# Slot weights in two halves: one batch of 8 matmuls ahead of a projection, the other behind it

## The reference

```python
xn = _layernorm(x, axis=-1)
q, k = _rope(hs @ Wq.T), _rope(hs @ Wk.T)       # per head, T = 256, DK = 128
A  = where(mask, einsum('bhtd,bhjd->bhtj', q, k) * scale, 0)
ok = enz * einsum('bhtj,bhjm->bhtm', A, es)     # es = exp(s), enz = exp(-cumlogsumexp(s)), m = 64 slots
qv = softmax(ok, axis=-1)
W2 = where(mask, einsum('bhtm,bhjm->bhtj', qv * enz, es), 0)
o  = einsum('bhtj,bhjd->bhtd', W2, v)
o_n = o * rsqrt(mean(o * o) + EPS) * g_norm_weight
out = (o_n * silu(hs @ Wg.T)) @ Wo.T
# ffn: gate, up and down projections with 4-bit weights and a tanh GELU
```

## Time and profile before

| | us |
|---|---|
| median of 3 runs | 1122.98 |
| lowest and highest | 1122.49, 1124.65 |
| the profiled execution's own time | 1122.49 |
| its span, first to last instruction | 1120.0 |
| mean granted TensorE clock, as a share of full speed | 0.985 |
| PE busy | 1084.0 (97%) |
| DVE busy | 928.1 (83%) |
| ACT busy | 650.6 (58%) |
| POOL busy | 425.5 (38%) |

### The profile page before, as it was taken

The page is one execution under the profiler, slowest core; times in us unless marked ns, Lnnn a source line. Parts: engine busy times, 40 slices in busy tenths (PEclk is TensorE's granted clock), DMA queues, the critical chain, the costliest instruction groups (busy, mean ns, idle before and its releaser), DMA issues.

```text
span 1120.0 us, 20624 instructions
## 1 busy us (share of the span) xinstructions
PE 1084.0 (97%) x7176; PEld 927.7 (83%) x7176; DVE 928.1 (83%) x1687; ACT 650.6 (58%) x2103; POOL 425.5 (38%) x308
## 2 busy tenths in 40 slices
PE   6888999999999999999999999999999999999996
PEld 5677888888888888888888888888888888888875
DVE  6788889888888889888888888888888898888863
ACT  4465566655655657555666656565665556655542
POOL 7142245432524345232453324443252334523231
PEclk9899999999999999999999999999999999999996
DMA  4002000020002000020000200011000200000001
GB/s 166 1 1 78 1 2 1 2 77 1 1 1 78 1 2 1 1 78 1 1 1 1 78 1 2 1 38 41 1 1 1 78 1 1 1 1 20 1 20 38
DMA packets 9526, 23.06 MB, mean 21 GB/s; under 512 B 848, under 2 KB 5840, under 8 KB 8528
## 3 DMA queue, kind: packets, MB, share of 16 engines
q1 hardware_dynamic: 9424, 21.76, 5.4%
HBM read 19.66 MB, written 2.10 MB: 19 GB/s over the span
## 4 chain that ended last, share of the span: by engine, by line
PE 84%; DVE 7%; issue 4%; POOL 2%; ACT 2%; DMA 0%; POOLq 0%; DVEq 0%; ACTq 0%
PE bank L205 20%; PE bank L207 19%; PE bank L206 19%; PE bank L303 4%; PE bank L366 4%; PE bank L316 3%; PE bank L337 3%; DVE xs L930 2%; PE bank L375 2%; PE bank L305 2%; PE bank L328 1%; PE bank L529 1%; PE bank L346 1%; PE bank L319 1%; PE bank L359 1%
## 5 line engine op out<-in xcount | busy, mean ns | idle before, releaser
L1200 POOL TENSOR_TENSOR inter_lo<-ffb,inter_hi 128x512 fp32r<-128x512 f32 x64 | 83.3, 1325 | 440.5 <-ACT inter_hi L678 440.5
L1191 POOL TENSOR_TENSOR qkT<-ra,xs 128x512 f32<-128x512 f32 x128 | 170.2, 1329 | 109.6 <-DVE xs L930 80.8
L640 ACT ACTIVATE sm<-bank,mx 128x64 f32<-128x64 f32 x256 | 76.5, 326 | 120.6 <-DVE mx L886 120.6
L930 DVE TENSOR_TENSOR xs<-xs,rope 128x512 f32<-128x512 f32 x128 | 129.5, 1012 | 0.0
L927 DVE TENSOR_TENSOR ra<-bank,rope 128x512 f32<-128x512 f32 x128 | 87.7, 685 | 46.9 <-ACT xs L622 44.7
L621 ACT ACTIVATE xs<-bank 64x512 f32<-64x512 f32 x128 | 76.2, 595 | 66.8 <-PE bank L207 43.8
L205 PE MATMUL bank<-xh,wqk_hi 128*128 128x512 f32 x256 | 109.9, 429 | 3.1 <-DVE h L990 2.6
L875 DVE RECIPROCAL enzT<-enzT 128x256 f32<-128x256 f32 x64 | 111.4, 1742 | 0.0
L205 PE MATMUL bank<-xh,wgu_hi 128*128 128x512 f32 x256 | 105.6, 412 | 0.0
L645 ACT ACTIVATE At<-bank 128x128 f32<-128x128 f32 x128 | 35.8, 281 | 114.1 <-DVE At L809 112.9
L205 PE MATMUL bank<-wvg_hi,xh 128*128 128x512 f32 x256 | 101.1, 395 | 1.0 <-DVE xl L978 1.0
(11 more groups left out here) (149 smaller groups left out, 3075.5 us busy)
## 6 DMA issues: line engine op xcount, KB each, us to landing
raw<-in_w_qkvg SPq DMA_DIRECT2D x7, 1024.0 KB, 5.0
scaled<-in_w_scaled SPq DMA_DIRECT2D x8, 640.0 KB, 7.1
packed<-in_w_packed SPq DMA_DIRECT2D x8, 384.0 KB, 5.7
acc<-in_x SPq DMA_DIRECT2D x4, 512.0 KB, 8.1
out<-acc SPq DMA_DIRECT2D x3, 512.0 KB, 2.9
raw<-in_w_qkvg SPq DMA_DIRECT2D x2, 512.0 KB, 7.1
out<-acc SPq DMA_DIRECT2D x2, 256.0 KB, 2.1
ws_raw<-in_w_slot SPq DMA_DIRECT2D x8, 48.0 KB, 1.8
```

What stands on the lines that cost most here:

```text
L640: ins = act.activation(sm[:, c], src[:, c], ACT.Exp, bias=mx[:, g:g + 1], accum_out=ssum[:, g:g + 1])
L930: dve.tensor_tensor(two(xs[i % 2][:, :]), two(xs[i % 2][:, :]), sin, ALU.mult).then_inc(sin_done, 1)
L1191: pool.tensor_tensor(qkT[:, i, :], ra[i % 2][:, :], xs[i % 2][:, :], ALU.add).then_inc(roped, 1)
L1200: pool.tensor_tensor(inter[1][e][:, :], ffb[e][:, :], inter[0][e][:, :].bitcast(F32), ALU.subtract).then_inc(inter_lo, 1)
```

## The change

`slot_weights` is called twice in a stage. Each call makes the weights of one batch entry, two token tiles for each of the two heads, and so half of the matmuls. The first call stands between the transposes of `esT` and `project_qk` 2, the second where the whole was, ahead of `carried`. `Wt` is four tiles of 128x256 in place of two of 128x512. Both halves use the first 256 columns of `sc[0]` and `sc[1]`, so PE's second half waits until DVE has read the first; in the last stage alone the second half goes to the banks `pj[2]` and `pj[3]`. DVE masks a half as soon as its place in the order comes: `weight_diagonal` 0 and 1 stand between `rope_sin` 0 and `rope_cos` 1, and 2 and 3 between `rope_sin` 1 and `rope_cos` 2. `W_full` and `W_diag` count in steps of four per stage.

```diff
-        Wt = [sb(f"Wt{h}", [P, NT, P]) for h in range(2)]
+        Wt = [sb(f"Wt{i}", [P, 2, P]) for i in range(4)]
...
+        def weight_bank(st, i):
+            return pj[i] if st == STEPS - 1 and i > 1 else sc[i % 2]
...
-            def slot_weights(st, bp):
-
-                for i in range(NT):
-                    t = slice(i * P, (i + 1) * P)
-                    for h in range(2):
-                        g = slice(h * M, (h + 1) * M)
-                        mm = pe.matmul(sc[h][:, t], esT[bp % 2][g, t], qe[g, t], start=True, stop=True)
-                mm.then_inc(W_full, 1)
+            def slot_weights(st, bp, b):
+
+                t0 = b * T
+                pair = [(weight_bank(st, 2 * b + h), slice(h * M, (h + 1) * M)) for h in range(2)]
+                for tt in range(2):
+                    t = slice(t0 + tt * P, t0 + (tt + 1) * P)
+                    for dst, g in pair:
+                        mm = pe.matmul(dst[:, tt * P:(tt + 1) * P], esT[bp % 2][g, t], qe[g, t], start=True, stop=True)
+                mm.then_inc(W_full, 2)
...
-                pe.wait_ge(W_diag, 2 * st + 1 + h)
+                pe.wait_ge(W_diag, 4 * st + 3 + h)
                 for i in range(NT):
-                    mm = pe.matmul(rg[h][:, i * DV:(i + 1) * DV], Wt[h][:, i, :],
+                    mm = pe.matmul(rg[h][:, i * DV:(i + 1) * DV], Wt[i // 2 * 2 + h][:, i % 2, :],
...
-                        pe.wait_ge(W_diag, 2 * st - 1 + i)
+                        pe.wait_ge(W_diag, 4 * st - 1 + i)
...
+                slot_weights(st, bp, 0)
                 if not last:
                     project_qk(st + 1, nbp, nhp, 2)
-                slot_weights(st, bp)
+                if last:
+                    pe.wait_ge(inter_done, 2 * STEPS)
+                else:
+                    pe.wait_ge(W_diag, 4 * st + 2)
+                slot_weights(st, bp, 1)
                 carried(st, last)
                 if last:
-                    pe.wait_ge(inter_done, 2 * STEPS)
                     pe.wait_ge(inter_lo, 2 * STEPS)
...
-            def weight_diagonal(st, h):
-                dve.wait_ge(W_full, st + 1)
+            def weight_diagonal(st, i):
+                dve.wait_ge(W_full, 4 * st + i + 1)
                 wait(dve, o_full, 2 * st)
-                src = sc[h][:, :].rearrange("p (n t) -> p n t", n=NT)
-                mask = mask_w[:, 0, :].unsqueeze(1).to_broadcast([P, NT, P])
-                dve.tensor_tensor(Wt[h][:, :, :], src, mask, ALU.mult).then_inc(W_diag, 1)
+                src = weight_bank(st, i)[:, 0:2 * P].rearrange("p (n t) -> p n t", n=2)
+                dve.tensor_tensor(Wt[i][:, :, :], src, mask_w[:, :, :], ALU.mult).then_inc(W_diag, 1)
...
-                wait(dve, W_full, n - 1)
+                wait(dve, W_full, 4 * (n - 1))
...
+                weight_diagonal(st, 0)
+                weight_diagonal(st, 1)
                 if not last:
                     rope_cos(st + 1, 1)
                     rope_sin(st + 1, 1)
-                weight_diagonal(st, 0)
-                weight_diagonal(st, 1)
+                weight_diagonal(st, 2)
+                weight_diagonal(st, 3)
```

## The result

| | before | after |
|---|---|---|
| median of 5 runs, us | 1122.98 | 1130.14 |
| lowest and highest, us | 1122.22, 1124.65 | 1129.09, 1133.07 |
| profiled execution, us | 1122.49 | 1129.53 |
| its span, us | 1120.0 | 1127.8 |

The changed kernel is slower, by less than 1%: the ratio is 1.0076, 95% interval 1.0056 to 1.0095, that is +8.5 us (6.3 to 10.7). The medians of the table lie 7.2 us apart. Of 15 executions of the changed kernel seven took 1127.5 to 1130.1 us, eight took 1132.8 to 1134.0 us, and none lies between; the median of the five in the table is one of the lower group, as is the profiled execution. The forecast was +9.2 us on the median, with 1132.2 us and a range of 1127.5 to 1136.5 us.

A forecast was written before the change was run, and what follows sets the result against it. PE's list was taken to bound the kernel; 8.6 us for 22 stages, 0.4 for the seven with bp = 3 and 0.5 for stages 0 and 1 made +9.5 us, median 1132.2 us, range 1127.5 to 1136.5.

The forecast's parts named there:

- What bounds the kernel: Mid-run, a stage lasts as long as PE's list takes to issue: PE busy 32.90 of 32.90 us.
- 0.39 us per visit: PE's added separate visit to the 64-row form between transposes and projection 2 costs 0.39 us beyond its matmuls.
- the step in behind a transpose: On PE, going from transposes into the 64-row form, shown by no row: 0.10 us taken, 0 to 0.20 possible.
- DVE's margin: DVE's first maskings end over 0.4 us before PE reaches its second half of the weights; priced at nothing.
- The stages with the split: Seven bp = 3 stages: PE's later arrival eats 0.33 us of waiting for POOL, leaving 0.06 each, 0.4 us in all.
- The sum inside the run: All terms over the stages together add +9.5 us, all of it inside the span.
- the 22 normal stages: Stages 2 to 30 without the seven of bp = 3: 0.39 us each, 8.6 us in all.
- stages 0 and 1: PE already waits for DVE there, hiding the step in; 0.2 to 0.3 us each remains, 0.5 us in all.
- The last stage: Stage 31: transposes and both halves stand side by side without a projection between, so no second visit; nothing added.
- A: Rival at PE's seams: the visit is cheaper than the rows say, +1 to +2 us, 1124.2 us; chance 0.08.
- B: Rival: PE waits for DVE's maskings, 8.7 us on top, 1140.9 us; chance 0.06.
- C: Rival: DVE's third sine starts before POOL's split, so seven PE waits go, -2.3 us, 1120.7 us; chance 0.04.

The follow-up runs named there:

- e1: Kernel before with PE's order kept and only DVE's two 128x512 maskings cut into four of 128x256 at the old place: 1123.54 us, ratio 1.0007.
- e2: Kernel before with only four of the eight weight matmuls moved ahead of projection 2 on PE, DVE's maskings unchanged: 1132.55 us, ratio 1.0079.
- e3: Kernel before plus one full-height dummy matmul over 128 rows between the transposes and projection 2: 1125.88 us, ratio 1.0030.
- e5: Kernel before with POOL's subtraction for the gate and up weights cut to 128x8 after the first head pair: 1120.30 us, ratio 0.9974.
- e8: Kernel before plus a pair of 64-row dummy matmuls directly behind slot_states, which has the 64-column form: 1136.60 us, ratio 1.0125.
- e7: Kernel before plus a pair of 64-column dummy matmuls over all 128 rows between the transposes and projection 2: 1137.55 us, ratio 1.0128.

## Why the prediction was right

- **What bounds the kernel**: PE's list. e1 and e2 show it: what DVE does in addition costs 0.4 us in the whole run, what PE's order adds is paid in full in every normal stage.
- **0.39 us per visit**: right, 0.39 to 0.40 in every normal stage. The term chosen by the nearest row, 0.10 us for the step in behind a transpose, is some 0.08 us in the profile after. The Trainium skill's rule ("TensorEngine Tiling (Array Packing)", "Tiling Modes", a change of mode drains the engine) agrees with the trace here, with e3 as its control: the price comes with the form and not with the place. A drain as such is not seen in a trace. What the page does not say is the price: 0.39 us there and back for the 64-row form, 0.34 for the 64-column form.
- **DVE's margin**: forecast "over 0.4 us" ahead of PE's second half, measured 0.44. The sine that was held up did swallow the delay.
- **The stages with the split**: this term was mis-sized. Forecast were 0.06 us left of each, +0.4 in all; measured are -0.5. In six of them nothing is left (33.41 us in both kernels in stage 11). The wait was read as 0.33 us; e5 shows that the long period held 0.50 us of cost in all, the part beyond the wait itself lying in slower passes behind it. The seventh, stage 19, was not looked at: it held 0.80 us and lost 0.41 with the change.
- **The sum inside the run**: forecast +9.5 us. The values of stage 30 start at 1070.44 and 1079.45 us, 9.0 apart. This is closer than the terms are: the 22 normal stages give 8.7 (forecast 8.6), the seven others -0.5 (0.4), stages 0 and 1 give 0.3 (0.5), and 0.5 us was there before the first divided group, at the transposes that start at 43.70 and 44.21 us, and has nothing to do with the change; that it fills half of the gap is luck:

```profile
1070.44 0.38 PE L366 MATMUL bank<-vS,Wt 128*128 128x128 f32 x2
```
```profile
1079.45 0.38 PE L370 MATMUL bank<-vS,Wt 128*128 128x128 f32 x2
```

- **The last stage** was forecast at nothing and gave 1.2 us back in this pair of traces (the spans differ by 7.8). This term was mis-sized, and not by the change: PE's clock. Windows over the same work in the last stage, before and after (the column behind POOL's is the granted clock):

```profile
1095.00:1101.00 6.00, 5.22 (x36) 4.59 (x35) 2.35 (x4) 0.00 (x0) 0.00 (x0) 0.51 0.26 87
```
```profile
1104.00:1110.00 6.00, 5.22 (x41) 4.59 (x40) 2.56 (x6) 0.00 (x0) 0.00 (x0) 0.61 0.26 87
```

PE had idled 3.7 us for the softmax just before in both, the clock fell to the lower of its two levels (1.2 GHz), and it came back sooner in the profile after, so that 41 passes in place of 36 start in the window. That is 0.5 us; the other 0.6 come from passes behind two later waits, which run at the lower level in before (from 1109.70 us on, granted clock 0.50 over 3 us) and begin at the upper one in after (from 1118.16 us on). The matmuls and the waits are the same in both, and the five runs of each kernel spread over 2.4 and 4.0 us, so I take this for a matter of the execution. With one trace of each kernel it is not shown. Of the 2.5 us by which the profiled pair (+7.0) stays under the forecast sum, 1.2 lie here, 0.5 in the stages before, and 0.8 outside the span, where the profiled execution of after has 1.7 us and that of before 2.5.
- **The rivals**: A and B are excluded by the profile after. C lost its race by 0.10 us in six stages and had its gain in the seventh; the prediction judged all seven by stage 11.

## What to carry to other kernels

Matmuls that split the array by rows or by columns are dear to visit: here a group in such a form between full-height matmuls cost 0.34 to 0.39 us of PE's time on top of its passes, and the 64-row form the same with four passes as with eight. Where PE is the bound, keep them in one block, next to another split form if there is one (0.23 us in place of 0.39 in e8), and read the price from the starts around an existing group. Here a delay on the bounding engine was hidden only where that engine already waited for a chain which the delay didn't move. And look at each stage of a kind, not at one: of seven like stages one went the other way.

## What the runs showed of the hardware

- A group in the 64-row form behind a projection: 0.10 us more before its first pass, 0.09 us more within it (put down to its start), 0.20 us more on the way out. In the 64-column form the round trip is 0.34 us (e7). From the 64-column form straight into the 64-row form and then out it is 0.23 us more than the former alone, beside the passes (e8).
- A DVE instruction with two operands in SBUF that meets POOL's ends 0.54 to 0.55 us after POOL's: 507.27 against 506.73, and 448.52 against 447.97 in the profile after, where it started 0.10 us behind and took 2.81 us in place of 0.7. Where the two started together, at 712.53 us in the profile after, it was POOL's that took longer, 2.90 us in place of 2.36, and DVE's took 0.68.
